# Attention row maxima: one turning matmul and four row-group matmuls in place of four scaled identities, the projections in one run, and new orders on every engine

## What is computed

```python
h = _layernorm(x) * (1 + ca) + sa
Q, K, V = ...                                   # 16 heads of 8 features
scores = einsum('bhqd,bhkd->bhqk', Q, K) / sqrt(8); masked outside |q - k| <= 32
attn = softmax(scores, axis=-1)
x = x + ga * (attn @ V) @ W_o
h = _layernorm(x) * (1 + cb) + sb
topk_idx, topk_weight = _gate(h, gate_weight, bias)          # 2 of 8 experts
y = sum over e of combine_w[:, e] * (silu(h @ gate_proj[e].T) * (h @ up_proj[e].T)) @ down_proj[e].T
x = x + gb * y
```

## Time and profile before

| | us |
|---|---|
| device time, median of 3 runs (164.87 to 165.09) | 164.94 |
| profiled execution, its own device time | 163.83 |
| its span, first to last instruction | 162.0 |
| PE busy in the span | 151.1 (93%) |
| DVE busy | 127.1 (78%) |
| ACT busy | 90.2 (56%) |
| POOL busy | 55.9 (34%) |

### The profile page before, as it was taken

One profiled execution on the slowest core, in us unless ns is written; L12 is line 12 of the kernel. 1 busy time (PEld: TensorE's weight loads), 2 busy tenths in 40 slices (PEclk: granted clock), 3 DMA queues, 4 the chain that ended last, 5 costly groups with the idle time before them and its releaser, 6 DMA issues.

```text
span 162.0 us, 5111 instructions
## 1 busy us (share of the span) xinstructions
PE 151.1 (93%) x1976; PEld 123.2 (76%) x1976; DVE 127.1 (78%) x353; ACT 90.2 (56%) x172; POOL 55.9 (34%) x109
## 2 busy tenths in 40 slices
PE   6799989999899999999999999999999999888993
PEld 2376778787677898978887888789888986674773
DVE  3439496495988999897999789877988898587872
ACT  3234387556666656575747764785166428624740
POOL 6420072021540606521662147212251306426340
PEclk9999999999999999999999999999999999999999
DMA  4874134034103503510351013401250000010002
GB/s 134 239 210 28 8 38 32 4 65 28 10 0 46 59 0 67 37 34 4 65 33 35 0 35 43 32 0 35 34 36 0 9 28 0 6 32 0 0 4 65
DMA packets 47431, 6.23 MB, mean 38 GB/s; under 512 B 42416, under 2 KB 47024, under 8 KB 47408
## 3 DMA queue, kind: packets, MB, share of 16 engines
q1 hardware_dynamic: 47264, 5.90, 23.4%
q10 hardware_dynamic: 144, 0.00, 0.0%
HBM read 3.81 MB, written 2.10 MB: 36 GB/s over the span
## 4 chain that ended last, share of the span: by engine, by line
PE 71%; issue 9%; ACT 8%; DVE 6%; POOL 4%; POOLq 0%; ACTq 0%; DVEq 0%
PE ps L763 11%; PE ps L797 11%; PE ps L863 10%; PE ps L778 5%; PE ps L856 5%; PE ps L921 3%; PE ps L839 3%; ACT probs L533 3%; PE ps L841 3%; PE ps L840 3%; PE ps L718 3%; PE ps L808 2%; PE ps L740 2%; PE ps L745 2%; PE ps L890 2%
## 5 line engine op out<-in xcount | busy, mean ns | idle before, releaser
L1160 DVE TRANSPOSE_TENSOR_REDUCE blkmax<-ps 128x44 f32<-128x1408 f32 x16 | 26.4, 1648 | 11.7 <-PE ps L770 9.5
L797 PEld LDWEIGHTS ps<-probs,v_bd 128*36 128x36 f32 x640 | 21.5, 113 | 7.4 <-issue 4.7
L533 ACT ACTIVATE probs<-ps 128x704 f32<-128x704 f32 x32 | 23.0, 755 | 6.1 <-PE ps L778 5.6
L797 PE MATMUL ps<-probs,v_bd 128*36 128x96 f32 (+2 forms) x640 | 25.1, 228 | 0.8 <-ACT probs L533 0.5
L359 POOL TENSOR_TENSOR act_w<-act,cw 128x512 f32<-128x512 f32 x15 | 15.7, 1044 | 21.7 <-issue 13.7
L763 PEld LDWEIGHTS ps<-q_sb,k_bd 32*128 32x128 f32 x640 | 19.3, 186 | 4.3 <-issue 2.4
L763 PE MATMUL ps<-q_sb,k_bd 32*128 32x96 f32 (+2 forms) x640 | 21.3, 274 | 0.7 <-ACT probs L533 0.5
L778 PE MATMUL ps<-shift,quad_ones 128*128 128x384 f32 x64 | 16.9, 370 | 0.0
L863 PE MATMUL ps<-wd_sb,act_t 128*128 128x128 f32 x128 | 16.2, 280 | 0.6
L863 PEld LDWEIGHTS ps<-wd_sb,act_t 128*128 128x128 f32 x128 | 15.0, 191 | 2.0 <-ACT act_t L557 1.8
L546 ACT ACTIVATE tanh_g<-ps 128x512 f32<-128x512 f32 x14 | 8.3, 596 | 14.4 <-PE ps L841 14.4
(11 more groups left out here) (108 smaller groups left out, 283.5 us busy)
## 6 DMA issues: line engine op xcount, KB each, us to landing
x_sb<-x SPq DMA_DIRECT2D x8, 128.0 KB, 3.2
v_spill<-v_sb SPq DMA_DIRECT2D x8, 128.0 KB, 2.3
v_bd<-v_spill SPq DMA_DIRECT2D x32, 32.0 KB, 3.1
out<-out_sb SPq DMA_DIRECT2D x7, 128.0 KB, 2.0
wgu_sb<-w_gu SPq DMA_DIRECT2D x1, 512.0 KB, 4.3
wm_sb<-wmod SPq DMA_DIRECT2D x1, 256.0 KB, 3.8
wd_sb<-w_down SPq DMA_DIRECT2D x1, 256.0 KB, 5.2
con<-consts SPq DMA_DIRECT2D x1, 244.0 KB, 3.2
```

The lines of the kernel that those rows point to most:

```text
L533: nc.scalar.activation(probs[:, t, hgs, cols], ps[:, hgs, cols], ACT.Exp, scale=float(DH) ** -0.5).then_inc(probs_ready, 1)
L797: last = nc.tensor.matmul(ps[p0:p0 + VW, OB, c0 + lo * KB:c0 + (hi + 1) * KB], v_bd[:, i % VB, kb, hg, :], view(probs[:, t, hg, at:at + 1] ...
L1160: nc.vector.tensor_reduce(blkmax[:, t, :, live(t):live(t) + LIVE], view(ps[:, 0, live(t) * KB:live(t) * KB + 1], [[BANK, NHG], [KB, LIVE], ...
```

## The change

It does these things:

- The row maxima are spread over a 128 x 128 tile (`spread_max`), turned by one float32 matmul of 32 columns into an unused stretch of bank 0 (`turn_max`), and multiplied with a -1/0 pattern of 128 x 128 elements out of PSUM (`shift_rows`, once per half). Then each head group has its own 32 partitions, and `subtract_max` is four matmuls of 32 contraction rows, one per row group and bank.
- K, Q and V are projected in one run (`project_qkv`), Q and V into one bank; q and k have two buffers each.
- The reciprocal and the product that make `cw` go from DVE to POOL (`expert_weights`).
- `x_sb` holds all eight images, and no load waits.
- Every engine's lists are in another order. The second `up` of an image, its second activation turn, the `weigh_values` of t = 1, `transpose_x1` and `logits` go into the next step. Most waits stand in the lists now, not in the helpers.

```diff
-XBUF = 4
+XBUF = B
...
+            def expert_weights(b):
+                wait(pool, wsum_ready, b, 1, 1)
+                nc.gpsimd.tensor_tensor(rsum[:], wsum2[:], minus_one[:], ALU.pow).then_inc(rsum_ready, 1)
+                wait(pool, rsum_ready, b, 1, 1)
+                nc.gpsimd.tensor_tensor(cw[:], wsel[:], view(rsum[:], [[1, NT], [0, E]]), ALU.mult).then_inc(cw_ready, 1)
...
+            def turn_max(i, t):
+                wait(pe, spread_ready, i, QT, t + 1)
+                nc.tensor.matmul(ps[:, 0, CELLS * KB:(CELLS + 1) * KB], max_by_head[:].rearrange("p h m -> p (h m)"),
+                                 con[:, C_REP:C_REP + KB], start=False, stop=True, skip_group_check=True)\
+                  .then_inc(turned_ps, 1)
+
             def subtract_max(i, t, pair):
-                wait(pe, shift_ready, i, PARTS, t * NPAIR + pair + 1)
+                wait(pe, shift_ready, i, QT, t + 1)
                 for hg in range(pair * PAIR, (pair + 1) * PAIR):
-                    last = nc.tensor.matmul(ps[:, hg, 0:CELLS * KB], quad_ones[:],
-                                            view(shift[:, hg, 0:1], [[0, 3], [1, QBT * KB]]),
+                    rows = slice(hg * KB, (hg + 1) * KB)
+                    last = nc.tensor.matmul(ps[:, hg, 0:CELLS * KB], head_ones[rows],
+                                            view(shift[rows, 0, 0:1], [[0, 3], [1, QBT * KB]]),
                                             start=False, stop=True, skip_group_check=True)
                 last.then_inc(shifted_ps, 1)
...
-            def shift_rows(i, t, pair):
+            def spread_max(i, t):
                 wait(dve, rowmax_ready, i, QT, t + 1)
+                wait(dve, turned_ps, i, QT, t)
+                nc.vector.tensor_tensor(
+                    view(max_by_head[:, 0, 0:1], [[KB, NHG], [QBT, G], [1, QBT]]),
+                    view(row_max[:, 0, 0:1], [[QBT, NHG], [0, G], [1, QBT]]),
+                    view(con[:, C_DEN:C_DEN + 1], [[0, NHG], [1, G], [0, QBT]]), ALU.mult).then_inc(spread_ready, 1)
+
+            def shift_rows(i, t):
+                wait(dve, turned_ps, i, QT, t + 1)
                 wait(dve, shifted_ps, i, PARTS, t * NPAIR)
                 nc.vector.tensor_tensor(
-                    shift[:, pair * PAIR:(pair + 1) * PAIR].rearrange("p h (q k) -> p (h q) k", k=KB),
-                    view(row_max[:, pair * PAIR, 0:1], [[1, PAIR * QBT], [0, KB]]),
-                    view(con[:, C_NI:C_NI + 1], [[0, PAIR * QBT], [1, KB]]), ALU.mult).then_inc(shift_ready, 1)
+                    shift[:], view(ps[:, 0, CELLS * KB:CELLS * KB + 1], [[0, QBT], [1, KB]]),
+                    view(con[:, C_QB:C_QB + 1], [[1, QBT], [0, KB]]), ALU.mult).then_inc(shift_ready, 1)
```

More of the change, by code:

```diff
@@ L319, in _ @@
             step(B - 2)
-            for b in range(B - 4, B - 1):
+            for b in range(B - 1 - 4, B - 1):
                 sp.wait_ge(out_ready, b + 1)
@@ new lines, in second_step, with third_step @@
+                weigh_values(1, 1, 0)
+            def third_step():
+                wait(pe, probs_ready, 1, PARTS, 4)
+                scores(2, 0)
+                weigh_values(1, 1, 1)
+                transpose_x1(0)
+                gates_part(3)
+                logits(0)
+                turn_max(2, 0)
+                wait(pe, ex_ready, 0, 1, 1)
+                transpose_o(1)
+                transpose_x(3)
+                subtract_max(2, 0, 0)
+                subtract_max(2, 0, 1)
+                wait(pe, on_ready, 1, 1, 1)
+                project_qkv(3)
+                wait(pe, probs_ready, 2, PARTS, 2)
+                scores(2, 1)
+                wait(pe, k_ready, 3, 1, 1)
+                transpose_on(1)
+                pe.wait_ge(gate_row_ready, 4)
+                up(0, 0)
+                turn_max(2, 1)
@@ L1008, in seventh_step @@
+                scores(B - 2, 1)
+                wait(pe, actt_ready, B - 5, NT, 2)
+                down(B - 5, 0)
+                transpose_on(B - 3)
+                down(B - 5, 1)
+                wait(pe, ont_ready, B - 3, 1, 1)
+                project_qkv(B - 1)
+                turn_max(B - 2, 1)
                 up(B - 4, 0)
+                wait(pe, k_ready, B - 1, 1, 1)
                 output_projection(B - 3)
-                project_v(B - 1)
-                scores(B - 2, 1)
-                project_k(B - 1)
@@ L1013, in seventh_step, with last_step @@
-                project_q(B - 1)
-                weigh_values(B - 2, 0, 0)
-                up(B - 4, 1)
                 subtract_max(B - 2, 1, 0)
                 subtract_max(B - 2, 1, 1)
+                wait(pe, v_kept, B - 1, 1, 1)
+                weigh_values(B - 2, 0, 0)
                 weigh_values(B - 2, 0, 1)
+            def last_step():
+                wait(pe, probs_ready, B - 2, PARTS, 4)
+                scores(B - 1, 0)
+                wait(pe, act_ready, B - 4, NT, 1)
+                up(B - 4, 1)
@@ L1019, in seventh_step @@
                 weigh_values(B - 2, 1, 0)
-                scores(B - 1, 0)
+                weigh_values(B - 2, 1, 1)
                 transpose_x1(B - 3)
+                wait(pe, act_ready, B - 4, NT, 2)
                 transpose_act(B - 4, 0)
-                weigh_values(B - 2, 1, 1)
-            def last_step():
+                turn_max(B - 1, 0)
                 logits(B - 3)
@@ L1279, in normalise_o @@
                 wait(dve, ot_ps, i, 1, 1)
+                wait(dve, ont_ps, i, 1, 0)
                 nc.vector.reciprocal(
@@ L1400, in third_step @@
-                row_maximum(2, 1)
-                shift_rows(2, 1, 0)
-                shift_rows(2, 1, 1)
-                gate(0, 1)
-                gated(0, 1)
+                gated(0, 0)
                 route_weights(0)
-                keep_k(3)
-                route_compare(1)
-                route_beats(1)
             def seventh_step():
```

597 lines of the change are left out of this document (285 added, 312 removed).

## The result

| | before | after |
|---|---|---|
| device time, median, us | 164.97 (4 runs, 164.87 to 165.09) | 169.31 (4 runs, 167.14 to 175.27) |
| profiled execution: its own time, span, us | 163.83, 162.0 | 169.59, 167.5 |
| mean granted clock of the profiled execution | 1.000 | 0.969 |

The changed kernel takes 1.0222 times as long, with a 95% interval of 1.0152 to 1.0291. It is slower by more than its interval, though not surely by as much as 2%; the prediction was 162.9 and faster.

What follows compares the result with a forecast made beforehand. PE was taken to bound the steady steps, the softmax cycle after the change. Sum: 10.28 + 41.4 + 4 x 16.2 + 25.8 + 17.7 = 160.0 span against 162.0, median 162.9; range 159.5 to 165.4.

Steps and rivals of the forecast that it cites:

- Ramp: Images 0 to 2: 45.05 us before the change, forecast at 41.4 after it.
- "slower" rival: Second norm's xn2 comes 0.45 late, each step and ramp half behind it pays: 3.2 us, median 166.1; chance 0.14.
- the tie that I had seen: Next step: xn2 laid out as ready at 2.85, where PE wants it at 2.83; 0.02 apart.
- The start: Term of 10.28 us ahead of the ramp in the sum.
- Steady period: Steps 3 to 6: from 16.8 to 16.2 us each, bound by the softmax cycle in the first half.
- PE idles 0.6: First half of a steady step: PE has 6.8 us of work and idles 0.6.
- PE stays the bound: Rival: the step is PE's work, 15.9 or 15.4 us; span 156.5, median 159.4; chance 0.2.
- Subtraction: Four matmuls in row groups per half: 0.36 us instead of 0.8, with 0.1 for entering; bounds 0.25 and 0.8.
- Turn: New matmul turning the maxima: 0.2 us of PE, 0.5 from the spread's end to its own.
- Expert weights on POOL: Power 0.711 us, product some 0.2; no cost in steady steps, 0.3 more ahead of cw in the last image.
- Modulation ahead of the scores: Ramp: the modulation now standing ahead of the first scores adds 0.4 us.
- Tail: After image 7: last residual starts 0.7 us sooner, so 18.37 becomes 17.7.

Runs made afterwards that it cites:

- start_filled: pool_wo_first with PE's two idle gaps at the start filled by four more idle matmuls: 162.72 us, ratio 0.9941.
- up_short_first: start_filled with one of three products left out of up(i - 3, 1), behind the first scores, in steps 3 to 5: 162.31 us.
- same_again: The changed kernel run once more with no edit: 168.01 us, ratio 1.0214.
- fill_the_wait: The changed kernel with 13 idle matmuls on PE ahead of the first output projection, the wait itself left: 167.28 us, ratio 1.0168.
- pool_wo_first: The changed kernel with scale_wo(0) moved ahead of scale_x(4) in POOL's second step: 164.25 us, ratio 0.9971.
- act_xn_early: The changed kernel with norm1_apply(3) put ahead of keep_on(0) and keep_gates(2) in ACT's second step: 164.27 us, ratio 0.9977.
- start_filled_scores_first: start_filled with the second modulation moved from ahead of the first scores to behind image 1's turns of x: 162.57 us, ratio 0.9919.
- weights_on_vector: start_filled with the expert weights' reciprocal and product back on DVE instead of POOL: 163.53 us, ratio 0.9988.

## Why the prediction was wrong

- **The failed step is the ramp**, the term of 41.4 that measured 46.91, under *Ramp*: "laid out call by call it came to 41.2". I laid out PE's and DVE's lists; a wait of PE for POOL has no term in that sum, so it stood at nothing without a reason, and I did not walk POOL's and ACT's lists of the second step. There the change put `scale_wo(0)` behind `scale_x(4)` and `norm1_apply(3)` behind `keep_gates(2)`. Either alone is harmless; both close a chain of 3.24 us in front of the output projection. Shown by two edits that each open it (168.01 to 164.25 and to 164.27), which bring the ramp to the 41.58 of the profile, 0.2 from my term. My "slower" rival was a different wait. It cost nothing in the steps, but the tie that I had seen is real: in start_filled xn2 is ready 2.81 into step 3, where PE takes it at 2.86 (2.51 against 2.85 in the next), and up_short_first ran into it. One wait for it shows, 0.16 in the drain of the profile after (142.98).
- **The price of an idle PE** was missing. I priced every stall by its length. The 3.1 us cost 2.1 more by the clock in the profile after, and 1.2 in same_again; fill_the_wait takes the clock's part away and leaves the wait.
- **The start** was taken as unchanged, 10.28. Both kernels have two groups of times, 1.2 us apart in pool_wo_first and 1.0 in the kernel before. Among the changed kernel's profiles the first scores start at 10.50 or at 12.00. The base of my sum was a profile at a lower time and the median of the runs an upper one; the 1.11 between them, which I added as a constant, has the size of that distance. Shortening the gaps makes the upper group rare. But their length does not sort the profiles: the start was slow with gaps of 0.93 and 0.63 (after), 0.79 and 0.63 (pool_wo_first) and even 0.50 and 0.20 (act_xn_early), and fast with 0.70 and 0.62 (same_again). What decides in a given execution stays open.
- **Steady period** 16.2: right, 16.22. But the mechanism was only half right, and the number in part luck. "PE idles 0.6" was wrong: PE is busy for 48.30 of 48.67, 16.1 a step where I had 15.9. Its runs fill the 7.32 of the first half, of which at most the 0.19 at the logits is waiting; my 6.8 is not itemised, so which run it had too short is not on record. The forecast was a step bound by the softmax cycle in its first half. The subtraction there does follow the shift by 0.05, but PE's work arrives with it, and no run shows the chain of the maxima alone to be the bound: of the 0.46 taken from PE, 0.17 a step came back, and the rest was the wait for xn2. The rival "PE stays the bound" holds for the second half (0.46 of 0.46 given back).
- **Subtraction** 0.36 per half, with the entry in it: 0.38 from start to start, and 0.18 instead of 0.1 to enter behind full matmuls, so 0.56 in the second half, which saves PE 0.32 and not 0.44. The Trainium skill, "TensorEngine Tiling (Array Packing)", section on tiling modes, says that a change of tiling mode drains TensorE, and gives no size; the 0.54 against 0.36 in front of the subtraction agrees that a change costs something. The row groups gain 0.5 a step with that paid. Without them the new form is slower than the kernel before (1.0106, 1.0034 to 1.0178).
- **Turn** 0.2: 0.24 of PE in the first half, 0.14 in the second; spread 0.22 in the steps (0.25), shift 0.29 (0.29), projections in one run 1.31 (1.39).
- **Expert weights on POOL**: power 0.70, product 0.22, as costed; but the move gained 0.4 and was not neutral. The Trainium skill, "GPSIMD Engine Reference", section on engine selection, would leave elementwise work to VectorE, as about twice as slow on GpSimd. The durations lean that way: 0.70 and 0.22 on POOL, 0.17 and 0.18 on DVE (there a reciprocal, not a power). The time did not: DVE's pair stood ahead of a block maximum, the 0.9 of POOL ahead of nothing that was late.
- **Modulation ahead of the scores** 0.4: 0.14. **Step 6** took 16.65 for 16.2 and **image 7** 25.40 for 25.8; the two misses cancel in the table above. **Tail** 17.7: 17.87.
- Of the 2.0 us that I forecast, 1.5 are in the span of start_filled (160.5), and 1.1 in the medians. The time around the span is 2.1 us in all profiles of the changed form and 1.8 in those of before; why, no run shows.

## What to carry to other kernels

Where a change rewrites the lists of in-order engines, walk every list, the lightly used ones first: an engine at 37% busy stopped the one at 91%, because an urgent call stood behind one whose wait went round by two other engines back to PE. A wait is harmless by what stands behind it and not by its length: POOL's 4.5 us wait cost 5.3 us in one profile and 4.4 in another and, after one call was moved, nothing. And a steady state right to 0.1 us says nothing of the ramp, whose lists are others. A right period does not show that the step is bound by what one thought, either: take a known amount of work out of it and see what the engine waits for then.

## What the runs showed of the hardware

- Around one idle stretch of 3.1 us on PE the granted clock falls to 0.50 and stays there while PE is busy again: from 38.3 to about 45.2 us in the profile after (PE idle from 36.2 to 39.26), from 39.1 to about 42.5 in same_again (idle from 34.7 to 37.75). Such a stretch cost its length and 1.2 to 2.1 us more.
- Gaps of 0.93 and 0.63 us at the start are followed by the same fall (0.50 from 8 to 10 us) in some executions and not in others: same_again, with the same code, had gaps of 0.70 and 0.62, and 1.00 there. With the gaps shortened by four short matmuls, 30 of 36 executions of the changed form (start_filled, start_filled_scores_first, weights_on_vector) lay in the lower group, in place of 7 of 24 (pool_wo_first, act_xn_early), and 12 of 12 of the kernel before in place of 23 of 35.
- The granted clock of a profile can read 1.00 where matmuls run at half speed: 1.19 for two of K in act_xn_early, 0.67 elsewhere.
- Work of PE in row groups of 32: four float32 matmuls of 384 columns start to start in 0.37 to 0.38 us, 0.81 to 0.87 over the full array, and 0.18 to enter behind full matmuls.
